# Layer 0 of two attention layers: transposing the softmax by VectorE blocks and a DRAM round trip

## The reference

```python
Bm = einsum('oc,bcn->bon', Wb, xf); Cm = einsum('oc,bcn->bon', Wc, xf); Dm = einsum('oc,bcn->bon', Wd, xf)
S = softmax(einsum('bcn,bcm->bnm', Bm, Cm), axis=-1)
att = einsum('bcm,bnm->bcn', Dm, S)
x = gamma * att + x
```

## Time and profile before

| | us |
|---|---|
| runs | 725.45, 719.98, 724.05; median 724.05 |
| profiled execution | 723.44 |
| its span, first to last instruction | 721.7 |
| TensorE busy in the span | 699.7 |
| VectorE busy | 536.8 |
| ScalarE busy | 455.3 |
| GpSimd busy | 229.9 |

### The profile page before, as it was taken

How to read it: one execution, slowest core, us unless ns; L and a number is a source line. 1 busy time by engine, 2 the same in 40 slices (tenths; PEclk the granted TensorE clock), 3 DMA queues, 4 the chain that set the end, 5 groups by cost and what they waited for, 6 DMA issues and landing times.

```text
span 721.7 us, 11880 instructions
## 1 busy us (share of the span) xinstructions
PE 699.7 (97%) x3888; PEld 592.7 (82%) x3888; DVE 536.8 (74%) x878; ACT 455.3 (63%) x820; POOL 229.9 (32%) x214
## 2 busy tenths in 40 slices
PE   5999999999999899999999999999999999999996
PEld 4888888888888677887888887887887888888885
DVE  3665465456547536999888889888889988889994
ACT  4552254145226415798777788877779877778883
POOL 0120021022013202356433356523346533334531
PEclk9999999999999999999999999999999999999999
DMA  8000210040130173700266400165501155501010
GB/s 275 2 2 29 96 50 15 29 131 0 44 131 1 30 175 99 194 1 1 57 148 148 116 30 31 45 152 127 145 15 44 35 122 126 126 16 45 10 45 35
DMA packets 29100, 52.72 MB, mean 73 GB/s; under 512 B 3456, under 2 KB 5760, under 8 KB 29056
## 3 DMA queue, kind: packets, MB, share of 16 engines
q1 hardware_dynamic: 29056, 52.19, 26.1%
HBM read 18.62 MB, written 8.39 MB: 37 GB/s over the span
## 4 chain that ended last, share of the span: by engine, by line
PE 88%; DVE 5%; ACT 3%; issue 3%; DMA 1%; SPq 0%; ACTq 0%; DVEq 0%
PE acc L1092 45%; PE scores L1092 26%; PE trans L1126 18%; DVE negmax L774 2%; DVE pt_lo L792 2%; ACT prob L581 1%; ACT pt_hi L591 1%; DMA x_raw<-in_x 1%; DVE o_sum L995 0%; ACT o_sum L695 0%; DVE x_lo L872 0%; ACT h_hi L639 0%; ACT x_hi L602 0%; DVE gn_sqdev L828 0%; DVE rsum L779 0%
## 5 line engine op out<-in xcount | busy, mean ns | idle before, releaser
L501 POOL TENSOR_SCALAR prob<-prob,rsum 128x1024 f32<-128x1024 f32 x159 | 179.8, 1131 | 474.5 <-DVE rsum L779 474.5
L591 ACT ACTIVATE pt_hi<-trans 128x512 fp32r<-128x512 f32 x320 | 175.0, 595 | 135.8 <-PE trans L1126 133.4
L774 DVE TENSOR_REDUCE negmax<-scores 128x1 f32<-128x1024 f32 x160 | 194.2, 1214 | 45.5 <-PE scores L1092 44.1
L792 DVE TENSOR_TENSOR pt_lo<-trans,pt_hi 128x512 fp32r<-128x512 f32 x320 | 204.4, 680 | 11.1 <-ACT pt_hi L591 10.7
L581 ACT ACTIVATE prob<-scores,negmax 128x1024 f32<-128x1024 f32 x160 | 179.2, 1120 | 30.1 <-DVE negmax L774 28.5
L1126 PEld LDWEIGHTS trans<-ident,prob 128*128 128x128 f32 x1280 | 146.9, 140 | 32.4 <-DVE pt_lo L792 5.1
L1126 PE MATMUL trans<-ident,prob 128*128 128x128 f32 x1280 | 168.8, 274 | 3.8 <-DVE pt_lo L792 3.3
L1092 PE MATMUL scores<-k_st,q_st 128*128 128x512 f32 x512 | 137.6, 391 | 0.0
L1092 PEld LDWEIGHTS scores<-k_st,q_st 128*128 128x128 f32 x512 | 95.9, 188 | 20.8 <-ACT prob L581 0.2
L1092 PE MATMUL acc<-pt_hi,v_st 128*128 128x512 f32 (+1 forms) x264 | 106.7, 407 | 1.8 <-DVE pt_lo L792 1.8
L1092 PE MATMUL acc<-pt_lo,v_st 128*128 128x512 f32 (+1 forms) x264 | 101.0, 385 | 0.0
(11 more groups left out here) (119 smaller groups left out, 890.6 us busy)
## 6 DMA issues: line engine op xcount, KB each, us to landing
k_st<-qk SPq DMA_DIRECT2D x64, 256.0 KB, 4.6
q_st<-qk SPq DMA_DIRECT2D x64, 128.0 KB, 2.4
x_raw<-in_x SPq DMA_DIRECT2D x8, 512.0 KB, 7.1
y_out<-in_x SPq DMA_DIRECT2D x16, 256.0 KB, 3.6
y_scratch<-y_out SPq DMA_DIRECT2D x16, 256.0 KB, 2.0
y_in<-y_scratch SPq DMA_DIRECT2D x4, 1024.0 KB, 7.2
y_res<-y_scratch SPq DMA_DIRECT2D x16, 256.0 KB, 3.6
out<-y_res SPq DMA_DIRECT2D x16, 256.0 KB, 2.0
```

Of the source, the lines that this page charges most:

```text
L501: nc.gpsimd.tensor_scalar(p, p, rsum[:, t % 2:t % 2 + 1], 1.0, ALU.mult, ALU.mult)\
L591: nc.scalar.activation(pt_block(pt_hi, (t // 4) % 2, t, h), trans[:, h, :].rearrange("p (j n) -> p j n", n=P), ACT.Copy).then_inc(pt_high, 1)
L774: nc.vector.tensor_reduce(negmax[:, t % 2:t % 2 + 1], scores[:, t % 2, :], AX_X, ALU.max, negate=True).then_inc(max_ready, 1)
L792: nc.vector.tensor_tensor(pt_block(pt_lo, slot, t, h), trans[:, h, :].rearrange("p (j n) -> p j n", n=P), pt_block(pt_hi, slot, t, h).bitc ...
```

## The change

In layer 0 alone, TensorE no longer transposes. Per tile:

- VectorE's `turn` transposes the 32x32 blocks of `prob` into `turned` (two buffers), with the blocks in another order.
- SyncE's `move_turned` stores `turned` (512 KB) to a DRAM tensor `turn_scratch`, waits for the store to land, and loads it back by four DMAs of 32 partitions x 4 rows x 1 KB, which put each block into its final partitions, into `pt_lo`.
- ScalarE's `turn_high_of` rounds `pt_lo` to `pt_hi` (128x1024, SBUF to SBUF); then `pt_lo` becomes `pt_lo - pt_hi` in place: on GpSimd for tiles 0, 1, 2 of each half (`POOL_LOWS`), on VectorE for the fourth (`DVE_LOW`).

`pt_hi` and `pt_lo` now hold queries and key blocks interleaved, so an AV matmul reads its 512 moving columns as 16 runs of 32 elements, 256 elements apart (`turned_keys`). The freed `trans` banks become a third buffer for scores, and `prob` gets four buffers. `av2` and `av3` of an image (tiles 4 to 7) are issued in the next image's steps 0 to 3, in halves, between its scores; the D groups move to steps 4 to 7; `av0` comes in four parts, each of which waits for one D group. The first image is unrolled from the loops. VectorE computes `result` of `prev_av2` and `prev_av3` in steps 2 and 4. `y_out`'s residual is loaded in two halves. The first group-norm set covers images 0 and 1 in place of 0 to 2, the second images 2 and 3.

The diff, cut to its core:

```diff
-D_STEPS = [1, 2, 4, 5]
-TAIL0 = ["av0", "t6", ("av1", 0, 2), "t7", ("av1", 1, 2), "av2", "next_a0", ("av3", 0, 3), "next_a1",
...
+SCORES0 = [("prev_av2", 0, 2), ("prev_av2", 1, 2), ("prev_av3", 0, 2), ("prev_av3", 1, 2), "d0", "d1", "d2", "d3"]
+D_STEPS = [4, 5, 6, 7]
...
+FIRST_HALF = [("av0", 0, 4), ("av0", 1, 4), ("av0", 2, 4), ("av0", 3, 4)]
+TAIL0 = FIRST_HALF + ["av1", "next_a0", "next_a1", "next_a2", "next_a3"]
+TAIL0_LAST = FIRST_HALF + [("av1", 0, 2), "next_qk0", ("av1", 1, 2), "next_qk1", ("av2", 0, 3), "next_qk2",
+                           ("av2", 1, 3), "next_qk3", ("av2", 2, 3), ("av3", 0, 2), ("av3", 1, 2), "next_qk4",
+                           "s0", "next_qk5", "s1"]
...
+HIGH_BEHIND = 2
+POOL_LOWS, DVE_LOW = (0, 1, 2), 3
...
-GN_SETS = [(0, IMAGES - 1), (IMAGES - 1, IMAGES)]
+GN_SETS = [(0, IMAGES - 2), (IMAGES - 2, IMAGES)]
...
+        def score_tile(t):
+
+            return scores[:, t % 3, :] if t % 3 < 2 else trans[:, :, :].rearrange("p a b -> p (a b)")
...
+        def turned_keys(buf, half, j):
+
+            rows = buf[:, half, :, :].rearrange("p j n -> p (j n)")
+            return rows.rearrange("p (m j c) -> p m j c", j=NT, c=QUAD)[:, :, j, :]
+
+        def turn_difference(engine, t):
+
+            return engine.tensor_tensor(turned_tile(pt_lo, t), turned_tile(pt_lo, t).bitcast(F32),
+                                        turned_tile(pt_hi, t).bitcast(F32), ALU.subtract)
...
+            def move_turned(i, t):
+
+                sp.wait_ge(turn_ready, TURN_CREDIT + T0_IMAGE * i + t + 1)
+                sp.dma_start(turn_dram[t], turned[:, t % 2, :]).then_inc(turn_stored[t % 2], 16)
+                sp.wait_ge(turn_stored[t % 2], 16 * ((T0_IMAGE // 2) * i + t // 2 + 1))
+                blocks = turn_dram[t].rearrange("(q c) (g n) -> g c q n", q=QUADS, g=QUADS)
+                for g in range(QUADS):
+                    dst = turned_tile(pt_lo, t).bitcast(F32)[g * QUAD:(g + 1) * QUAD, :]
+                    sp.dma_start(dst.rearrange("c (q n) -> c q n", q=QUADS), blocks[g]).then_inc(turn_moved[t % 4], 16)
...
+            def image0(i, last):
+                t0 = T0_IMAGE * i
+                for t in range(T0_IMAGE):
+                    if last and t == 2:
+                        norm_root(0)
+                    normalise0(t0, t)
+                    if t - 3 in POOL_LOWS:
+                        turn_low_of(t0, t - 3)
+                    if last and t in NORM_STEPS0:
+                        norm_chunk(0, NORM_STEPS0.index(t))
+                for t in POOL_LOWS:
+                    turn_low_of(t0, t + 4)
...
+            def turn_high_of(i, t):
+                act.wait_ge(turn_moved[t % 4], TURN_DMA * (2 * i + t // 4 + 1))
+                nc.scalar.activation(turned_tile(pt_hi, t), turned_tile(pt_lo, t).bitcast(F32), ACT.Copy)\
+                    .then_inc(turn_high, 1)
...
+            def turn(i, t):
+
+                dve.wait_ge(prob_ready, T0_IMAGE * i + t + 1)
...
+                nc.vector.transpose(turned[:, t % 2, :],
+                                    prob_tile(t).rearrange("p (j g c) -> p g j c", g=QUADS, c=QUAD))\
+                    .then_inc(turn_ready, 1)
...
                 for s in range(T0_IMAGE):
                     if s >= 1:
-                        recip(t0, s - 1)
-                    row_max(t0, s)
+                        recip0(t0, s - 1)
+                    if s in (2, 4) and not first:
+                        result(f"prev_av{2 + s // 4}", i - 1)
+                    if 1 <= s <= 4:
+                        turn(i, s - 1)
+                    row_max0(t0, s)
...
+                    if s == HIGH_BEHIND + 4:
+                        turn_low_of(t0, DVE_LOW)
+                    if s > 4:
+                        turn(i, s - 1)
...
                 def scores0(s):
-                    pe.wait_ge(exp_ready, t0 + s + 1)
+                    pe.wait_ge(exp_ready, t0 + s + (1 if s < 2 else 0))
...
+                def values(name, of, part, parts):
...
-                        pe.wait_ge(pt_split, SPLIT_CREDIT + 2 * t0 + 8 * (half + 1))
+                        pe.wait_ge(turn_low_pool, 6 * of + 3 * (half + 1))
+                        pe.wait_ge(turn_low, 2 * of + half + 1)
+                    if name == "av0":
+                        evacuated(plan.number(f"d{part}"))
...
-                    if s >= LAG:
-                        transpose_tile(t0, s - LAG)
                     if s in D_STEPS:
                         project_d(D_STEPS.index(s))
-                evacuated(plan.number("d3"))
+                    elif not first:
+                        values(SCORES0[s][0], i - 1, *SCORES0[s][1:])
```

More of the change, by code:

```diff
@@ L173, in plan0 @@
 def plan0(i, last=False):
-    return Plan("layer0_last") if last else Plan("layer0", i)
+    if last:
+        return Plan("layer0_last")
+    return Plan("layer0_first") if isinstance(i, int) and i == 0 else Plan("layer0", i - 1)
 def plan1(i):
@@ L419, in image0 @@
                     load_x(i + 1)
-                for name in plan.names:
+                for t in range(T0_IMAGE):
+                    if t == 4 and not first:
+                        store_result(i - 1, 3)
+                        sp.wait_ge(y_stored, FREE_CREDIT + i * 64)
+                        load_result_residual(i, 1)
+                    move_turned(i, t)
+                    if t == 1 and not first:
+                        store_result(i - 1, 2)
+                for name in ends(TAIL0_LAST if last else TAIL0):
                     if name.startswith("next_qk"):
@@ L658, in image0 @@
                         high(d_part(d_hi, n), plan, f"d{n}")
+                turn_high_of(i, 4)
+                if not last:
+                    for half in range(X_HALVES):
+                        x_part_high(i + 1, half)
+                turn_high_of(i, 5)
+                turn_high_of(i, 6)
                 for name in ends(TAIL0_LAST if last else TAIL0):
@@ L662, in image0 @@
                         exp(T1_BASE, 0)
-                    elif name.startswith("t"):
-                        trans(n)
-                        if name == "t7" and not last:
-                            for half in range(X_HALVES):
-                                x_part_high(i + 1, half)
                     elif name.startswith("next_a"):
@@ L951, in image0 @@
                         norm_next(0)
-                recip(t0, T0_IMAGE - 1)
+                recip0(t0, T0_IMAGE - 1)
+                low(d_part(d_lo, 3), d_part(d_hi, 3), plan, "d3", highs + plan.until("d3", KINDS0))
+                turn(i, T0_IMAGE - 1)
                 if last:
-                    norm_low(3)
+                    for c in range(4):
+                        norm_low(c)
+                else:
+                    for half in range(X_HALVES):
+                        x_part_low(i + 1, half)
                 for name in ends(TAIL0_LAST if last else TAIL0):
@@ L960, in image0 @@
                         row_max(T1_BASE, n)
-                    elif name.startswith("t"):
-                        trans_low(t0, n)
-                        if name == "t7" and not last:
-                            for half in range(X_HALVES):
-                                x_part_low(i + 1, half)
                     elif name.startswith("av"):
-                        result(n)
+                        result(name, i)
                     elif name.startswith("next_a"):
```

202 lines of the change are left out of this document (127 added, 75 removed).

## The result

The changed kernel takes 733.97 us (median of 4 runs, 732.63 to 735.88) where the kernel before took 723.57 beside it: ratio 1.0146, 95% interval 1.0108 to 1.0185. It is slower, outside the 1% that the prediction gave to "no change", and inside its widest range (700 to 738).

What follows compares the result with a forecast made beforehand. TensorE, busy 97% of the span, was taken as layer 0's bound. Images (-7.8, -12.6, +5.4), lock (+3) and clock (+2) sum to -10.0 us: 723.4 to 713.4, median 714.0; range 700 to 738.

Steps and rivals of the forecast that it cites:

- c: SyncE's time per tile in layer 0 for store, wait and four load issues: 5.0 us, with ends 4.6 and 6.6.
- I take 2.8 in all: SyncE's issue of a 512 KB store and the wait for it to land, worked from a 256 KB store: 2.8 us.
- up to c = 5.5: Middle image: tile 7 is ready before the next image's prev_av2 wants it, as long as c is at most 5.5 us.
- rival 1: SyncE's queue becomes the bound: c = 6.2, AV halves 2.8 us late in four images, +22, 736 us; chance 0.18.
- For tiles 4 to 7 SyncE starts at 31.8: Middle image: SyncE starts these tiles 31.8 us in, needs 4c = 20, so the last load lands at 54.
- wanted at 58.3: Middle image: the next image's prev_av2 needs tile 7 at 55.6 + 2.7 = 58.3 us; its subtraction ends at 56.4.
- the lock and the clock: Two added costs in layer 0: VectorE subtractions blocked beside GpSimd's, +3 us; TensorE's lower clock after two long waits, +2.
- about 10 us are lost: First image: TensorE could begin av0 at 27.5 and begins at 37.7; the image ends at 54.1, -7.8 us.
- rival 2: VectorE's block transpose of four-byte elements runs at half rate, 2.3 us: +5 per image, +20, 734 us; chance 0.08.
- Rival 3: Every VectorE subtraction (tile 3, tile 7, x low) is blocked by GpSimd, up to 2.6 us each: +9, 723; chance 0.10.
- 0.7 + 0.8 was taken: Before av0 in a middle image: 0.7 us wait for D group 2's low half, plus 0.8 per image from the lock.
- Rival 4: AV's moving operand, read in runs of 32 elements 1 KB apart, costs a tenth more: +9, 723 us; chance 0.09.

Runs made afterwards that it cites:

- the best kernel: The changed kernel with the store issued one tile ahead on SyncE in steps 5 to 7 and the first image's D groups in steps 0 to 3: 714.43 us, 0.9887.

## Why the prediction failed, by its own steps

**The step that failed is c, SyncE's time per tile: "I take 2.8 in all"** for the store and its wait, and with it the claim that a middle image holds "up to c = 5.5". The four issues were priced at 2.2 us and took 1.73, 0.43 each. The wait was worked out from a lone 256 KB store and came to 2.8; a lone store here takes indeed 2.7. But in steps 4 to 7 most stores are not alone: they follow loads, and take 3.6 to 5.0. So c is 5.3 to 6.8, not 5.0, and 5.9, 5.6 and 6.1 on average in the second, third and last image. A latency was read from a row where the queue was empty and used where it is full. The range of c (4.6 to 6.6) was right but for one tile, and so was the statement that the gain is gone from 5.8 on. The value in it was chosen near the good end, and the chance of rival 1 (0.18) was too small for a term with so little room: 0.5 us between 5.0 and 5.5.

**Two more premises of that step did not hold.** "For tiles 4 to 7 SyncE starts at 31.8": it starts at 34.9, since the exchange of `y_out` that stands ahead in its queue, and takes 4.0 us there, had no time in the prediction. And the first to be late is not `prev_av2`, wanted at 58.3, but an A group that TensorE is ready for 54.6 us into the image, by way of ScalarE's order. In the second image ScalarE can copy tile 7 at 61.4, where the last load was to land at 54: 3.1 us of the 7.4 are the start, 3.7 are c (four tiles), 0.6 the landing. No run takes off the start alone; it is just as late (34.7) in the best kernel, whose middle images take 57.6, so without the wait it does no visible harm.

**The sum by images.** Predicted 54.1, 55.6, 55.6 and 74.9; measured 58.5, 63.4, 61.0 and 84.1: 26.8 us more, from which come off the 5.0 that the prediction added for the lock and the clock. 21.8 is the distance from -10.0 to +11.8. Running without SyncE's wait gave 54.9, 57.6, 57.6 and 73.7, 23.2 us less (19.8 by the medians). That takes away the whole wait and not only the part by which c was short, but it brings the images to within 3.6 us of the forecast ones, and the forecast had no loss from SyncE.

**The first image.** 7.8 us were to be saved and 3.4 were. The idle time was foreseen: "about 10 us are lost" ahead of `av0`, and TensorE's four waits there are 0.62, 0.71, 5.94 and 2.35, 9.6 in all. The 4.4 us are slower matmuls. The D group behind the wait of 5.94 and the first matmuls of `av0` behind that of 2.35 ran at the low clock (0.21 in place of 0.12 apart, and 0.43 in place of 0.24). By the prices of the earlier trace rows, D groups and scores took 2.6 us too long, AV 2.1, of which 0.5 are the strided operand, and the A groups 0.4; the waits were 0.6 shorter. The sum carried 1.2 for the clock elsewhere. What the prediction missed is that the idle time could be had back: with the D groups early, and the store one tile ahead, the image is 54.1, where the store ahead alone gives 56.2.

**What was right.** Half of rival 1: four tiles in a row fall behind on SyncE, and its 736 is 2 us off. But its c of 6.2 came from issues at 3.4 us and a wait of 2.8; the issues took 1.73 and the wait was the long part, and its sum had no low clock. The nearness of the number is luck. The block transpose was priced well, and rival 2 falls:

```profile
L902 DVE STREAM_TRANSPOSE turned<-prob_more 128x1024 f32<-128x1024 f32 x16 | 19.8, 1237 | 17.7 <-DMA turn_scratch<-turned 9.9 <-POOL prob_more L576 7.8
...
L398 POOL TENSOR_TENSOR pt_lo<-pt_lo,pt_hi 128x1024 fp32r<-128x1024 f32 x24 | 57.9, 2412 | 32.0 <-ACT pt_hi L678 32.0
...
L398 DVE TENSOR_TENSOR pt_lo<-pt_lo,pt_hi 128x1024 fp32r<-128x1024 f32 x8 | 11.0, 1375 | 12.8 <-ACT pt_hi L678 12.8
```

1.24 us against 1.22 taken; GpSimd's subtraction 2.41 against 2.6. The wait ahead of `av2` in the last image came to 4.6 us against 4.2, though 6 us later than the prediction placed it. The transposes went, 64 an image, and the AV that was put off reappeared in the last image.

**Rival 3, the lock,** is real and small. VectorE's subtraction took 1.375 us on average, 0.15 over the 1.22 of the earlier trace rows. In the second image GpSimd subtracts from 124.25 for 2.39 us, until 126.64. VectorE's two `x_lo`, from 125.60, take 3.26 in place of 2.44, while its block transpose at 124.43, with one input, took its usual 1.25 beside the same GpSimd instruction. The Trainium skill (SBUF — State Buffer, Who interferes with whom) states that a VectorE instruction with two SBUF inputs is locked out while a GpSimd instruction reads SBUF, and one with a single SBUF input, outside its two-port modes, is not. These rows agree with it: 0.82 us over, where GpSimd had 1.04 left. In the middle images TensorE's wait for `d_lo` ahead of `av0` is 1.0 us, where 0.7 + 0.8 was taken, so on TensorE's path the lock cost at most some 0.3 us per image.

**Rival 4, strided moving operands,** is there at about half of its assumed price, if the stride is the reason. TensorE in the third image of the best kernel, 12 AV matmuls and then 12 score matmuls:

```profile
134.14 0.40 PE L1241 MATMUL acc<-pt_hi,d_hi 128*128 128x512 f32 x1
...
136.98 0.39 PE L1241 MATMUL scores<-x_hi,a_hi 128*128 128x512 f32 x1
...
139.73 0.40 PE L1241 MATMUL acc<-pt_hi,d_hi 128*128 128x512 f32 x1
```

2.84 us and 2.75 us: 0.237 each against 0.229. The AV matmuls of the kernel before, with a contiguous operand, took 0.227. So it is 96 x 0.010 = 1.0 us per image. No run reads a contiguous operand in the new order, so that the stride is the reason is likely and not shown. By the timeline, 1.1 of the 2.0 us by which the middle image of the best kernel (57.6) exceeds the forecast (55.6) are AV; the A groups make 0.4, D groups and scores 0.3, waits 0.1.

## What to carry to other kernels

Before work is moved off a full engine onto a round trip store, wait, load, work out the pace of the queue that waits, with the latency of a store that follows other transfers, and not that of a lone one; if it is within a tenth of what the plan can bear, as here (5.0 against 5.5), take it as the bound. Count in that queue's other work too. The cure here was only an order, with the two buffers already there: issue the next store before waiting for the last one. It turned a loss of 1.5% into a gain of 0.7%, and of 1.1% with the early D groups, where the transposes alone were priced at 28 us. And where an engine works in order, look for what stands behind its new wait: here an A group, unrelated to the round trip, paid for it.

## What the runs showed of the hardware

- A store of 512 KB on SyncE's queue was followed by its dependent loads after 2.7 to 2.8 us when 1.2 us or more had passed since the issue before it, and after 3.4 to 5.0 when it was issued within 0.11 us of it, mostly behind four loads of 128 KB each. The Trainium skill (DMA: Bandwidth & Descriptors, Anatomy of one DMA) describes a DMA issued by GpSimd, and puts about 2 us of it on fixed costs whatever the size; its fit, 2.0 us plus the bytes at 436 GB/s, would give 3.2 us here, an estimate. The lone store lies between the two figures, and the page has no term for the 0.6 to 2.3 us that the company of earlier transfers adds.
- An issue of a load from DRAM into 32 partitions cost SyncE 0.43 us in most cases (1.73 for four), into 16 partitions 0.45 (3.58 for eight); cutting a transfer in two doubled its price in issues.
- A block transpose of 128x1024 four-byte elements took VectorE 1.24 us, what one pass over 1024 elements took (1.22); the one at 124.43, wholly beside a subtraction of GpSimd, took 1.25.
